# Expert rows gathered two groups ahead, and three runs of WKV 2's scans standing later in a four-layer kernel

## The reference, cut to what matters

```python
# WKV of layer l: decay d per channel and batch; k = v = the side input
a[t] = a[t-1] * d + exp(k[t]) * v[t]        # num, forward; the same backward
b[t] = b[t-1] * d + exp(k[t])               # den, forward; the same backward
c = sigmoid(x) * (num / max(den, 1e-8)) * (0.8 + 0.2 * tf)
...
# feed-forward of layer 1: 64 experts, 6 per token, at most CAP = 48 tokens per expert
buf = buf.at[se, slot].set(x[tok])                          # rows by expert
h = silu(einsum('ech,ehf->ecf', buf, w_gate)) * einsum('ech,ehf->ecf', buf, w_up)
out = einsum('ecf,efh->ech', h, w_down)
y = segment_sum(gathered * w, tok)                          # back to tokens
```

## Time and profile before

| | |
|---|---|
| median of 3 runs | 452.96 us (451.02 to 453.14) |
| the profiled execution | 450.25 us, its span 448.4 us |
| TensorE busy | 397.3 us, 89% of the span |
| VectorE busy | 357.7 us, 80% |
| ScalarE busy | 218.3 us, 49% |
| GpSimd busy | 105.1 us, 23% |
| mean granted TensorE clock | 0.960 of full speed |

### The profile page before, as it was taken

How to read it: one execution, slowest core, us unless ns; L and a number is a source line. 1 busy time by engine, 2 the same in 40 slices (tenths; PEclk the granted TensorE clock), 3 DMA queues, 4 the chain that set the end, 5 groups by cost and what they waited for, 6 DMA issues and landing times.

```text
span 448.4 us, 5081 instructions
## 1 busy us (share of the span) xinstructions
PE 397.3 (89%) x1664; PEld 214.9 (48%) x1664; DVE 357.7 (80%) x659; ACT 218.3 (49%) x406; POOL 105.1 (23%) x76
## 2 busy tenths in 40 slices
PE   0988999989993997989999999999999899997673
PEld 0433464676841465766776773444444344432221
DVE  4999979899699479898979879527977966559995
ACT  3774655681295275647765583521111141157770
POOL 1000004200000521232330000147684754440000
PEclk9999779999998598999999999999999999999897
DMA  7940000640078418875676530540000000000011
GB/s 259 401 181 1 2 0 0 238 174 1 0 244 273 101 45 233 233 248 179 204 191 212 219 117 1 205 170 1 0 1 0 1 0 0 1 0 0 1 48 47
DMA packets 12251, 47.45 MB, mean 106 GB/s; under 512 B 2897, under 2 KB 5434, under 8 KB 9794
## 3 DMA queue, kind: packets, MB, share of 16 engines
q1 hardware_dynamic: 11074, 43.20, 27.4%
q0 software_dynamic: 1152, 3.93, 3.9%
HBM read 44.76 MB, written 2.37 MB: 105 GB/s over the span
## 4 chain that ended last, share of the span: by engine, by line
PE 48%; DVE 27%; issue 14%; POOL 4%; DMA 3%; ACT 2%; SPq 0%; POOLq 0%; DVEq 0%
PE bank L1718 7%; PE bank L1705 6%; PE bank L1582 4%; POOL arena L389 4%; PE bank L1750 3%; PE bank L1747 3%; PE bank L1447 3%; PE bank L1400 2%; DMA arena<-token_rows,arena 2%; PE bank L1673 2%; PE bank L1498 2%; PE bank L1357 2%; DMA kT<-in_kT 2%; PE bank L1770 1%; PE bank L1611 1%
## 5 line engine op out<-in xcount | busy, mean ns | idle before, releaser
L686 ACT ACTIVATE early<-bank 128x512 f32<-128x512 f32 (+1 forms) x24 | 14.3, 597 | 86.0 <-PE bank L1718 76.6
L1582 PE MATMUL bank<-onehot,rows 128*128 128x512 f32 x192 | 51.8, 409 | 0.0
L1246 DVE TENSOR_TENSOR early<-early,bank 128x512 f32<-128x512 f32 (+1 forms) x24 | 16.4, 684 | 37.8 <-ACT early L686 33.3
L1718 PE MATMUL bank<-arena 128*128 128x512 f32 (+1 forms) x96 | 42.2, 600 | 0.1
L389 POOL DMA_INDIRECT arena<-token_rows,arena x24 | 27.5, 1145 | 58.6 <-PE bank L1620 52.7
L1582 PEld LDWEIGHTS bank<-onehot,rows 128*128 128x128 f32 x192 | 34.4, 191 | 10.3 <-issue 3.9
L1705 PE MATMUL bank<-cT,arena 128*128 128x512 f32 x80 | 37.9, 596 | 0.0
L400 POOL TENSOR_TENSOR early<-early,arena 128x512 f32<-128x512 f32 (+1 forms) x12 | 20.1, 1672 | 62.6 <-DMA arena<-pair_weights 55.7
L406 POOL TENSOR_TENSOR early<-early,arena 128x512 f32<-128x512 f32 x10 | 22.3, 2228 | 29.3 <-DVE early L1246 29.3
L1718 PEld LDWEIGHTS bank<-arena 128*128 128x128 f32 (+1 forms) x96 | 15.7, 181 | 22.6 <-issue 21.2
L1065 DVE TENSOR_SCALAR onehot<-const,arena 128x1024 fp32r<-128x1024 f32 x24 | 18.0, 752 | 9.7 <-PE bank L1582 9.2
(11 more groups left out here) (371 smaller groups left out, 872.3 us busy)
## 6 DMA issues: line engine op xcount, KB each, us to landing
arena<-in_w_gateup SPq DMA_DIRECT2D x16, 768.0 KB, 6.3
arena<-in_w_down SPq DMA_DIRECT2D x8, 768.0 KB, 10.4
arena<-in_wq SPq DMA_DIRECT2D x1, 2048.0 KB
arena<-in_wo SPq DMA_DIRECT2D x1, 2048.0 KB, 7.9
const<-in_const SPq DMA_DIRECT2D x1, 1688.0 KB, 11.3
arena<-in_w_upgate SPq DMA_DIRECT2D x1, 1408.0 KB, 5.8
kT<-in_kT SPq DMA_DIRECT2D x2, 512.0 KB, 5.4
xT<-in_xT SPq DMA_DIRECT2D x1, 1024.0 KB, 9.0
```

The lines of the kernel that those rows point to most:

```text
L1582: return mm(bank[2 * ct + ch][:], rows1[:, i % RRING, part, ct * P:(ct + 1) * P], onehot1[:, t, ch * CHUNK:(ch + 1) * CHUNK], start=False, ...
L1718: last = mm(dst, (bup, bga)[z][:, f * P:f * P + fw], ((zu1, zg1), (zud, zgd))[k][z][:, ch * CHUNK:(ch + 1) * CHUNK], start=False, stop=Tru ...
```

## The change

The wait ahead of the gathers of group T now asks for the turned rows of group T - 3, so that from group 3 on the gathers are let go one group earlier; for group 2 the condition stays as it was. And three pieces of WKV 2's numerator stand later on VectorE: `forth(2, 1, 0)` moves from the tail of group 0 into the block of group 1, `forth(2, 1, 1)` from the block of group 1 to its tail, `back_again(2, 1, 1)` from the tail of group 1 into the block of group 2.

```diff
@@ -382,7 +382,7 @@
             pool.wait_ge(S("rows_out"), 48)
             for t in range(ST):
                 if t % GT == 0 and t >= 2 * GT:
-                    pool.wait_ge(S("h1_turned"), 2 * (t // GT - 1))
+                    pool.wait_ge(S("h1_turned"), 2 * max(t // GT - 2, 1))
                 if t >= XRING:
                     pool.wait_ge(S("xgT_done"), (t - XRING) // GT + 1)
                     pool.wait_ge(S("wslot_ready"), (t - XRING) // GT + 1)
@@ -1094,11 +1094,12 @@
                     den(2, 0)
                     den(2, 1)
                 if g == 1:
+                    forth(2, 1, 0)
                     back_again(2, 1, 0)
-                    forth(2, 1, 1)
                 if g == 2:
                     num_own(2, 0)
                     num_own(2, 1)
+                    back_again(2, 1, 1)
                     num(2, 0)
                     num(2, 1)
                 if g == 3:
@@ -1123,10 +1124,8 @@
                 for t in range(GT):
                     slot_rest(g, t)
 
-                if g == 0:
-                    forth(2, 1, 0)
                 if g == 1:
-                    back_again(2, 1, 1)
+                    forth(2, 1, 1)
                 if g == 2:
                     forth(3, 0, 0)
                 if g == 3:
```

## The result

The changed kernel took 450.17 us (median of 7 runs, 447.20 to 451.62) against 451.49 us for the kernel before (7 runs, 449.26 to 453.14); the ratio is 0.994, with a 95% interval of 0.991 to 0.997. That is 1.3 us between the medians and 2.7 us by the ratio, where 3.55 were forecast. When the same kernel was run once more beside the experiments, 12 runs against 35 gave 0.999 (0.996 to 1.002). Runs that took over 1.5% more than the fastest of their kernel are left out of every ratio here: one each in s1, s7 and s8, and four of nine in s4.

What follows compares the result with a forecast made beforehand. The expert loop was taken to be bound by TensorE except for stalls in groups 1, 3 and 6. Terms 4.16 - 1.55 + 0.22 + 0.72 = 3.55 us off 452.96 gave 449.4 us, range 447.9 to 450.9.

Steps and rivals of the forecast that it cites:

- The stall of group 1: Group 1: moving forth(2, 1, 0) starts L1085 2.58 us earlier and avoids 1.58 us of slower matmuls, worth 4.16 us.
- The wait for group 2's weights: Start of group 2: early gathers share the DMA engines, weights land at 181.8, TensorE waits 1.55 us.
- a sign of being wrong: Group 2's down weights landing before 180 or after 184 us would show the forecast wrong.
- Rival (B): Clock falls at the remaining stalls in group 2 or 3, 1.58 us each: 451.0 for one, 452.6 for both; chance 0.20.
- another of the signs: A lower granted clock anywhere from group 1 to group 3 would show the forecast wrong.
- The exchange of stalls in group 3: Group 3: the gather's wait goes and a 1.9 us wait on L1085 comes, 14.38 against 14.60 us, gaining 0.22.
- Group 6: Group 6: gathers let go one group earlier remove its wait, gaining 0.72 us.
- Rival (C): Group 1: group 2's own last gather lands late, TensorE idles and the clock falls; 452.3 us, no change; chance 0.08.
- one more of the signs of being wrong: A wait of TensorE at L1574 of group 1 would show the forecast wrong.
- Rival (D): Start of group 2: weights land 22.0 us after issue, a 10.2 us wait plus clock; slower, 459.7 us; chance 0.05.
- The sum: Whole kernel: 4.16 - 1.55 + 0.22 + 0.72 = 3.55 us gained, 449.4 us against the median of 452.96.

Runs made afterwards that it cites:

- s1: The changed kernel with all gathers let go as before the change, so only the scans moved; 0.989 of the time of the kernel before.
- s7: The changed kernel with group 3's gathers as before, later ones released by gate_up(T - 2), and VectorE's pieces spread over groups 3 to 7; 0.992 against the kernel before.
- s8: The kernel before, with three idle matmuls where TensorE waits for L1085 in group 1; 0.999 against the kernel before.
- s4: The changed kernel with three idle matmuls ahead of group 2's first matmuls; 0.997 against the kernel before.
- s3: The changed kernel with gathers let go early only from group 5 on; 0.992 against the kernel before.
- s2: The kernel before with only the change's earlier gathers, the scans where they were; 0.993 against the kernel before.
- s5: The changed kernel with forth(3, 0, 0) also moved, from the tail of group 2 into group 3's block; 1.002 against the kernel before.
- s6: The changed kernel itself, unaltered, profiled and timed once more; 0.999 against the kernel before.
- t1: The changed kernel with group 2's third gather waiting for the semaphore that releases the weights, group 3's gathers as before the change; 1.002 against the kernel before.
- t2: The changed kernel with group 2's third gather waiting for the semaphore that releases the weights, group 3's gathers early; 1.001 against the kernel before.

## Why the prediction was right, and where it was off

- **The stall of group 1** (4.16 us): right. Without the wait that followed, group 1 took 15.36 - 2.51 = 12.85 us, 4.14 less than before, and 12.82 in s3. Both halves hold: L1619 came 2.67 us earlier against its group's start, and s8 measured the clock's half at 1.54 to 1.58.
- **The wait for group 2's weights** (1.55 us): right in kind and place, mis-sized. It was 2.51, as the landing took 14.2 us and not 13.3. The term took one landing of 10.7 as a fixed base and added the gathers. The base itself varies: 11.7 and 13.1 in two executions of the same order (s3, s1). What the gathers add, 2.6 us in the sum, no run shows by itself: s2 has 12.6 with three of them beside. The landing at 184.8 is also behind the 184 that was named as a sign of being wrong.
- **Rival (B), the clock**, came true at that wait: 1.68 us, and with it another of the signs. An idle time of 2.51 us let the clock fall, and 1.9, 1.63 (s1), 1.53 and 1.47 did not. The length alone doesn't decide it: 2.06 us let it fall in group 4 of s5 (0.63 behind the wait), and 2.13 us in group 3 of s8 did not (1.00). Together the two cost 4.19 us instead of 1.55, which is where the forecast of this execution went. A loop 3.55 us shorter was forecast and it was 1.2 us shorter.
- **The exchange of stalls in group 3** (0.22 us): right, 0.33. L1085 came later than its place before by the amount foreseen, L1619 5.02 us behind the group's start where 5.21 was worked out. s5 shows that the wait belongs to VectorE's list.
- **Group 6** (0.72 us): right, 0.84, and group 5 another 0.12.
- **Rival (C)**, which had 8 chances in 100, was underrated. It is in no row of the first profile after, but in s6's of the same program. My reason against it (group 3's gathers stand behind it in its queue) was true and beside the point, as t1 and t2 show: what matters is whether the gather is out before the weights, and that hangs on half a microsecond between its issue and L769, which in these profiles goes with the clock ahead of the loop. The wait at L1573 of group 1 in s6 is one more of the signs of being wrong. With the old stall in group 1, such a gather had 2.6 us more before anybody waited for it.
- **Rival (D)** rests on a misread row. The 22.0 us of the earlier trace rows belong to another transfer, the 1 MB of layer 0's down weights, issued at 7.2 us by L286; the slowest of the loop's own loads is the 13.7 of the earlier trace rows, and the longest seen in any run for group 2's is the 14.2 here.
- **The sum**, 3.55 us, was right in sign and order for the first measurement (2.7 us by the ratio), and that is luck in part. The two profiled executions of the changed kernel have a loop 1.2 us shorter and 2.4 us longer than before, the second gets about 2 us back just ahead of the loop, and neither gives 2.7. The forecast of 449.4 was also counted from 452.96, the median of three runs; the seven beside the result have 451.49. The two measurements, 0.994 and 0.999, mix such executions. How often the kernel before has the late gather, and what it costs there, stays open: its two profiles (with s8) don't have it, and the changed kernel's times, 447.2 to 452.9, don't fall into clear sets.

## What to carry to other kernels

A stall that is removed takes the slack of everything behind it along: go through the transfers that are wanted next, and set their landing, with its scatter over executions, against the new time. Let a gather out early by a condition that puts it ahead of bulk transfers and of long VectorE instructions, not merely by one that comes earlier; and look twice at those that would run beside a load that somebody is about to wait for, though what they cost it isn't shown here. When one profile fits the forecast and the times don't, profile the same program again, and lay the two over each other from before the stretch in question: here the cause lay ahead of it.

## What the runs showed of the hardware that I had not expected

- One gather of 164 KB landed 3 to 5 us after the start of its issue when it went out ahead of the weights, and 8.3, 8.7 and 10.1 us after it when it went out behind them, with 2.36 MB of weights in flight (t1, t2, s4). Counted from the end of the issue it is 7.4 us in all three.
- A gather's issue on GpSimd took 0.95 us where nothing held it up and 1.97 to 2.65 beside L769 in the traces shown here. The earlier trace rows has one of 1.96 as well, from 191.72 to 193.68, and it ends 0.8 us behind an L779, a sum with both inputs in SBUF (191.65 to 192.87). A start of L769 just before or just behind the issue decides which gather it hits (166.10 against 166.60; 168.05 against 167.98).
- The same program's granted clock fell or stayed in different places in two executions: in group 2 in the one, in group 1 in the other. It also came back at different times ahead of the loop (0.61 and 0.72 on average over the same instructions), and in the execution in which it came back sooner, the third gather of group 2 was held up beside L769, in the other one of group 3.
